# Ranking and expert stages of a graph layer: sums between the halves of a split, TensorE's experts written out, statistics moved to ScalarE

## The reference, cut to what matters

```python
xn = layernorm(x)                                    # x: 6250 nodes x 256
x = x + gnn(xn, src, dst, edge_weight) + mix(xn)     # 100000 edges, sorted by dst
x = x + ffn(layernorm(x))

def gnn(x, row, col, val):       # row = src, col = dst
    agg = segment_sum(val[:, None] * x[col], row, num_segments=6250)
    return agg @ W.T + b

def ffn(x):                      # 8 experts, hidden size 1024, the best 2 of each token
    scores = x @ Wg.T + bg
    combine = softmax over the top 2, 0 for the other experts
    for e in range(8):
        h = relu(x @ W1[e].T + b1[e])
        out += combine[..., e:e+1] * (h @ W2[e].T + b2[e])
```

## Time and profile before

| | |
|---|---|
| median of 3 runs | 2398.07 us (2395.67 to 2400.01) |
| the profiled execution's own time | 2397.73 us |
| its span, first to last instruction | 2395.8 us |
| TensorE busy, share of the span | 1732.4 us, 72% |
| TensorE weight loads | 1202.8 us, 50% |
| VectorE | 1504.8 us, 63% |
| ScalarE | 1248.6 us, 52% |
| GpSimd | 1546.4 us, 65% |
| mean granted TensorE clock | 0.838 of full |

### The profile page before, as it was taken

One profiled execution on the slowest core, in us unless ns is written; L12 is line 12 of the kernel. 1 busy time (PEld: TensorE's weight loads), 2 busy tenths in 40 slices (PEclk: granted clock), 3 DMA queues, 4 the chain that ended last, 5 costly groups with the idle time before them and its releaser, 6 DMA issues. The chain is left out here.

```text
span 2395.8 us, 56194 instructions
## 1 busy us (share of the span) xinstructions
PE 1732.4 (72%) x13448; PEld 1202.8 (50%) x13449; DVE 1504.8 (63%) x3574; ACT 1248.6 (52%) x4045; POOL 1546.4 (65%) x1870
## 2 busy tenths in 40 slices
PE   4876636666666777777666666575899999999994
PEld 2355534444443555555222222365677777777773
DVE  8898826666666776766666676657344544544542
ACT  0044426666666666666666676340455555555552
POOL 3048866777777777777777777104466666666662
PEclk8988868999998999999655555555899999999997
DMA  4012215555555544443333454240222222222224
GB/s 147 1 58 70 68 51 172 156 157 156 152 154 153 152 120 120 121 121 113 104 102 116 142 169 125 93 158 4 51 41 42 42 41 41 43 41 41 42 42 127
DMA packets 140509, 230.72 MB, mean 96 GB/s; under 512 B 33192, under 2 KB 94916, under 8 KB 140214
## 3 DMA queue, kind: packets, MB, share of 16 engines
q0 software_dynamic: 67040, 147.18, 24.5%
q1 hardware_dynamic: 73398, 82.71, 11.1%
HBM read 187.80 MB, written 48.38 MB: 99 GB/s over the span
## 5 line engine op out<-in xcount | busy, mean ns | idle before, releaser
L952 POOL DMA_INDIRECT misc<-z_d,consts x902 | 859.4, 953 | 252.1 <-issue 226.5
L1204 DVE SCALAR_TENSOR_TENSOR acc<-ps,consts,acc 128x256 f32 x902 | 434.8, 482 | 298.7 <-PE ps L1286 281.6
L1675 PE MATMUL ps<-big,rec 128*128 x840 | 314.2, 381 | 39.1 <-DVE rec L1802 33.4
L1284 PE MATMUL ps<-misc 128*128 128x256 f16 x565 | 176.3, 312 | 221.9 <-ACT rec L983 99.9
L1661 PE MATMUL ps<-misc,big 128*128 128x128 f16 x1680 | 324.7, 221 | 0.0
L1659 PE MATMUL ps<-misc,big 128*128 128x128 f16 x1680 | 324.4, 221 | 0.3 <-ACT misc L1773 0.3
L1660 PE MATMUL ps<-misc,big 128*128 128x128 f16 x1680 | 323.1, 220 | 0.0
L1800 DVE CAST rec<-misc 128x512 f16<-128x512 f32 x210 | 98.0, 466 | 342.1 <-ACT misc L1694 269.0
L983 ACT ACTIVATE rec<-rec,misc 128x128 f16<-128x128 f16 x674 | 230.2, 392 | 155.7 <-DVE rec L1065 154.8
L983 ACT ACTIVATE misc<-rec,misc 128x128 f16<-128x128 f16 x678 | 231.4, 392 | 93.5 <-DVE rec L1065 91.4
L1284 PEld LDWEIGHTS ps<-misc 128*128 128x128 f16 x565 | 57.3, 101 | 365.7 <-ACT rec L983 173.1
(11 more groups left out here) (337 smaller groups left out, 3988.5 us busy)
## 6 DMA issues: line engine op xcount, KB each, us to landing
big<-in_w2T SPq DMA_DIRECT2D x60, 256.0 KB, 2.9
misc<-z_d,consts POOLq DMA_INDIRECT x902, 2.8
big<-xT_d SPq DMA_DIRECT2D x98, 128.0 KB
big<-in_w1T SPq DMA_DIRECT2D x32, 256.0 KB, 2.8
tok_d<-misc SPq DMA_DIRECT2D x50, 132.0 KB, 1.7
y_d<-acc SPq DMA_DIRECT2D x50, 128.0 KB, 1.7
xT_d<-misc SPq DMA_DIRECT2D x49, 128.0 KB
z_d<-misc SPq DMA_DIRECT2D x49, 128.0 KB, 1.7
```

Source lines behind the costliest of these rows:

```text
L952: e.indirect_dma_start(out=rows[k], out_offset=None, in_=c.z_d, in_offset=bass.IndirectOffsetOnAxis(ap=idx[u][:, k:k + 1], axis=0)).then_i ...
L1204: e.scalar_tensor_tensor(out=rows_of, in0=out_ps[t % BG], scalar=c.gain, in1=rows_of, op0=ALU.mult, op1=ALU.add).then_inc(s_add[k], 1)
L1284: e.matmul(o, w[:, 0, :], rows[k][:, 0:D], start=True, stop=False)
L1675: l = e.matmul(y_ps[s.u], high[s.u][:, m, :], c.w2[:, bass.ds(at, 2 * D)], start=m == 0, stop=m == HB - 1)
```

## The change

In `rank`: `src` has a semaphore of its own (`s_src`), and VectorE's one-hots wait for it alone; the one-hots and TensorE's counts are written out for 49 blocks. `pick1` is made by ScalarE as a copy of the identity. The statistics of x are made by ScalarE: 49 sums with an accumulator output, a mean by VectorE at block 1 of the places loop, 49 sums of squares, and the remaining steps by VectorE at blocks 42, 45 and 46. The 28 indicators and `started` move to GpSimd, `blk_row` to ScalarE behind the places loop, TensorE's sum for it too. The places have three PSUM buffers instead of two, and the reaches stand at blocks 5, 6, 8, 9 and so on to 45. In `route`, `c.experts` goes. In `experts`, VectorE makes the sums of tile i - 1 between the two halves of tile i; TensorE's program is written out, loads eight expert numbers before every eighth tile, and puts pair m behind group m.

```diff
@@ -233,6 +233,7 @@
+    prefix = [c.wide[u] for u in (1, 2, 0)]
...
@@ -276,11 +279,12 @@
         def _(e):
-            for t, a in inputs:
-                e.dma_start(t[:, 0:EF], a[0:EF * P].rearrange("(p t) -> p t", p=P)).then_inc(s_load, 16)
-            e.wait_ge(s_preset, 3)
-            for t, a in inputs:
-                e.dma_start(t[0:ER, EF:EF + 1], a[EF * P:E].rearrange("(p t) -> p t", t=1)).then_inc(s_load, 16)
+            for n, (t, a) in enumerate(inputs):
+                sem = s_load if n else s_src
+                e.dma_start(t[:, 0:EF], a[0:EF * P].rearrange("(p t) -> p t", p=P)).then_inc(sem, 16)
+                if n == 0:
+                    e.wait_ge(s_preset, 3)
+                e.dma_start(t[0:ER, EF:EF + 1], a[EF * P:E].rearrange("(p t) -> p t", t=1)).then_inc(sem, 16)
...
@@ -320,7 +324,6 @@
-            g.add(e.memset(pick1, 1.0))
...
@@ -337,12 +340,22 @@
-            select(pick1, pick1, ALU.is_equal, 0, [[-1, NT], [0, P]], 1)
...
+            e.wait_ge(s_end, 1)
+            g.sync()
+            e.tensor_scalar(started, tile_no, end[:, 0:1], None, ALU.is_ge).then_inc(s_started, 1)
+            e.wait_ge(s_delta, 1)
+
+            def indicate(n):
+                if n >= 2:
+                    e.wait_ge(s_dest, n - 1)
+                e.tensor_scalar(ind[n % 2], kio, first_run[:, n:n + 1], None, ALU.is_ge).then_inc(s_ind, 1)
+            for n in range(NG):
+                indicate(n)
...
@@ -379,22 +392,18 @@
-            e.wait_ge(s_load, 96)
+            e.wait_ge(s_src, 32)
...
-            with e.Fori(0, NT // 7) as i:
-                for u in range(7):
-                    b = i * 7 + u
-                    e.tensor_scalar(onehot[:, bass.ds(b, 1), :], one(blk16), number[:, bass.ds(b, 1)], None,
-                                    ALU.is_equal).then_inc(s_hot, 1)
+            for b in range(NT):
+                e.tensor_scalar(onehot[:, b, :], blk16, number[:, b:b + 1], None, ALU.is_equal).then_inc(s_hot, 1)
+            e.wait_ge(s_load, 64)
...
-            e.wait_ge(s_x, 32)
-            stats(e, v, c, st, c.mean, var, s_var)
...
@@ -403,9 +412,6 @@
-            e.wait_ge(s_std, 1)
-            v.link(e.reciprocal(c.rstd, std))
-            e.scalar_tensor_tensor(out=c.nbias, in0=c.mean, scalar=-1.0, in1=c.rstd, op0=ALU.mult, op1=ALU.mult).then_inc(s_norm, 1)
...
@@ -424,15 +430,15 @@
-            e.tensor_scalar(started, tile_no, end[:, 0:1], None, ALU.is_ge).then_inc(s_end, 1)
+            e.nop().then_inc(s_end, 1)
...
@@ -442,11 +448,23 @@
-            e.wait_ge(s_row, 1)
-            e.tensor_scalar(blk_row[0:1, :], row[0:1, 0:ET], float(D), None, ALU.mult).then_inc(s_blkrow, 1)
-            e.wait_ge(s_blkrow, 1)
             v.sync()
             e.nop().then_inc(s_base, 1)
+
+            def moments(n):
+                if n == 0:
+                    e.wait_ge(s_sums, 1)
+                    e.tensor_scalar(c.mean, st[:, :, 0], -1.0 / D, None, ALU.mult).then_inc(s_mean, 1)
+                elif n == 1:
+                    e.wait_ge(s_sums, 2)
+                    e.tensor_scalar(var, st[:, :, 1], 1.0 / D, EPS, ALU.mult, ALU.add).then_inc(s_var, 1)
+                elif n == 2:
+                    e.wait_ge(s_std, 1)
+                    v.add(e.reciprocal(c.rstd, std))
+                else:
+                    v.sync()
+                    e.wait_ge(s_mean, 1)
+                    e.tensor_tensor(c.nbias, c.mean, c.rstd, ALU.mult).then_inc(s_norm, 1)
...
@@ -465,16 +483,12 @@
-            def indicate(g):
-                if g >= 2:
-                    e.wait_ge(s_dest, g - 1)
-                e.tensor_scalar(ind[g % 2], kio, first_run[:, g:g + 1], None, ALU.is_ge).then_inc(s_ind, 1)
             for b in range(NT):
                 e.wait_ge(s_pre, b + 1)
-                e.copy_predicated(place, onehot[:, b, :].bitcast(U16), c.wide[b % 2 + 1][:, 0:EC]).then_inc(s_pos, 1)
-                if b < NG:
-                    indicate(b)
-                elif cleared <= b < cleared + 4:
+                e.copy_predicated(place, onehot[:, b, :].bitcast(U16), prefix[b % 3][:, 0:EC]).then_inc(s_pos, 1)
+                if b in (1, 42, 45, 46):
+                    moments((1, 42, 45, 46).index(b))
+                if cleared <= b < cleared + 4:
                     whole(b - cleared)
                 e.wait_ge(s_pos, b + 1)
...
@@ -517,6 +531,34 @@
         def _(e):
+            e.wait_ge(s_k, 2)
+            e.copy(pick1, c.ident[:, 0:NT].rearrange("p (t a) -> p t a", a=1).to_broadcast([P, NT, P])).then_inc(s_pick, 1)
...
+            junk = [matrix(a, 1, D) for a in xn] + [xT[0].rearrange("p h n -> p (h n)").rearrange("p (a d) -> p a d", a=1)]
+
+            def total(sem, n):
+                e.wait_ge(s_mean if n else s_x, 1 if n else 32)
+                e.nop().then_inc(sem, 2)
+                with e.Fori(0, NT // 7) as i:
+                    for u in range(7):
+                        at = bass.ds(i * 7 + u, 1)
+                        to = junk[2 if u == 6 else u % 2]
+                        e.wait_ge(sem, i * 7 + u + 1)
+                        if n == 0:
+                            l = e.activation(to, c.acc3[:, at, :], ACT.Copy, accum_out=st[:, at, 0])
+                        else:
+                            l = e.activation(to, c.acc3[:, at, :], ACT.Square, bias=c.mean[:, at], accum_out=st[:, at, 1])
+                        l.then_inc(sem, 1)
+                e.wait_ge(sem, NT + 2)
+                e.nop().then_inc(s_sums, 1)
+            total(s_sum[0], 0)
+            total(s_sum[1], 1)
+            e.wait_ge(s_scale, 1)
+            e.wait_ge(s_pos, cleared)
+            e.activation(pieces[:, 2, :, :], twice(wgt.bitcast(F32)), ACT.Copy, scale=c.gscale[:, 0:1]).then_inc(s_whi, 1)
+            e.wait_ge(s_int, 2)
+            e.copy(pieces[:, 0, :, :], twice(blk_i)).then_inc(s_piece, 1)
...
@@ -539,17 +581,14 @@
-            e.wait_ge(s_scale, 1)
...
+            e.wait_ge(s_row, 1)
+            e.activation(blk_row[0:1, :], row[0:1, 0:ET], ACT.Copy, scale=float(D)).then_inc(s_blkrow, 1)
             mask(Turn(0, 0))
...
@@ -577,17 +616,14 @@
-            with e.Fori(0, NT // 7) as i:
-                for u in range(7):
-                    b = i * 7 + u
-                    e.wait_ge(s_hot, b + 1)
-                    for x, y in cols:
-                        e.matmul(counts[:, x:y], band[:, bass.ds(P - 1 - b, P)], onehot[:, bass.ds(b, 1), x:y],
-                                 start=False, stop=False)
+            for b in range(NT):
+                e.wait_ge(s_hot, b + 1)
+                for x, y in cols:
+                    e.matmul(counts[:, x:y], band[:, P - 1 - b:2 * P - 1 - b], onehot[:, b, x:y], start=False, stop=False)
             for x, y in cols:
...
@@ -596,9 +632,6 @@
-            e.wait_ge(s_end, 1)
-            e.matmul(row[0:1, 0:512], few[:, 0:1], started[:, 0:512], start=True, stop=True)
-            e.matmul(row[0:1, 512:ET], few[:, 0:1], started[:, 512:ET], start=True, stop=True).then_inc(s_row, 1)
...
@@ -617,13 +650,13 @@
-                if b >= 2:
-                    e.wait_ge(s_pos, b - 1)
+                if b >= 3:
+                    e.wait_ge(s_pos, b - 2)
                 for x, y in cols:
-                    e.matmul(c.wide[b % 2 + 1][:, x:y], c.before, onehot[:, b, x:y], start=True, stop=False)
+                    e.matmul(prefix[b % 3][:, x:y], c.before, onehot[:, b, x:y], start=True, stop=False)
                 for part in (lo16, hi16):
                     for x, y in cols:
-                        l = e.matmul(c.wide[b % 2 + 1][:, x:y], pick1[:, b, :], part[:, x:y], start=False, stop=part is hi16)
+                        l = e.matmul(prefix[b % 3][:, x:y], pick1[:, b, :], part[:, x:y], start=False, stop=part is hi16)
                 l.then_inc(s_pre, 1)
...
@@ -633,10 +666,16 @@
+            e.wait_ge(s_pick, 1)
+            reached = [5 + g * 3 // 2 for g in range(NG)]
             for b in range(NT):
                 places(b)
-                if 1 <= b <= NG:
-                    reach(b - 1)
+                if b in reached:
+                    reach(reached.index(b))
+            e.wait_ge(s_pos, NT)
+            e.wait_ge(s_started, 1)
+            e.matmul(row[0:1, 0:512], few[:, 0:1], started[:, 0:512], start=True, stop=True)
+            e.matmul(row[0:1, 512:ET], few[:, 0:1], started[:, 512:ET], start=True, stop=True).then_inc(s_row, 1)
...
@@ -1309,7 +1348,6 @@
-    c.experts = matrix(pos.take(MT // 4 * 8, I32), MT // 4, 8)
...
@@ -1509,10 +1547,7 @@
-            v.link(e.memset(c.experts, 0))
-            for n in range(5):
-                v.add(e.tensor_copy(c.experts[:, :, n], order[:, n:n + MT - 4:4]))
-            v.add(e.tensor_copy(c.expert, order))
+            v.link(e.tensor_copy(c.expert, order))
...
@@ -1637,7 +1672,7 @@
-    BEHIND = ((), (), (0,), (1,), (2,), (3, 4), (5,), (6, 7))
+    KNOWN = 8
...
@@ -1793,6 +1828,8 @@
+                    if n and not s.zero:
```

(60 more changed lines are left out.)

3 lines of the change are left out of this document (2 added, 1 removed).

## The result

The changed kernel takes 2298.97 us (median of 4 runs, 2297.10 to 2301.28), the kernel before 2397.62 beside it: ratio 0.9589, 95% interval 0.9572 to 0.9605. The forecast was 2299, range 2284 to 2337. The profiled execution took 2297.7 us, its span is 2296.0, 99.8 less than before.

What follows compares the result with a forecast made beforehand. It took a loop between ScalarE and VectorE, 6.48 us a tile, to bound the experts, and VectorE to be ranking's path. 2397.7 - 71 (experts) - 1 (routing) - 27 (ranking) = 2298.7, forecast 2299, range 2284 to 2337.

Steps and rivals of the forecast that it cites:

- rival 6: Experts: the loop between ScalarE and VectorE isn't what bounds, so they stay as they are; -28 alone, 2370 us; chance 0.05.
- rival 4: Experts: GpSimd becomes the bound if its scatter and gather pair took 6.0 us; +36, 2335 us; chance 0.05.
- TensorE's pace: Experts: TensorE becomes the bound at 5.50 us a step, taken from one step that ran without a wait.
- Rival 1: Experts: TensorE's sequencer becomes the bound, each step losing 0.3 us; +31, 2330 us; chance 0.11.
- The load: Experts: loading expert numbers before every eighth tile costs TensorE 0.8 us each time, bounds 0.5 and 1.5.
- 102 x 5.65: Experts: the steps behind the turn at 1703.04, at 5.65 us each, take 576.3 us; with 11.8 before them, 588.1.
- TensorE's order: Experts: products starting after group 0 make a loop through TensorE of 5.0 us, below 5.50.
- What the statistics covered: Ranking: with statistics off VectorE, the gain's transfer and TensorE's transpose come back in part, +0.7 us.
- The wait at block 1: Ranking, places loop: VectorE stalls 5 us for ScalarE's 49 sums, bounds 0 and 18.
- Indicators: Ranking, places loop: GpSimd takes 0.8 us for each indicator of 512 elements, has 1.6, and keeps up.
- Rival 2: Ranking: indicators on GpSimd block VectorE's predicated copies, 28 x 0.8 to 1.5 us, part inside the stall; +20, 2319; chance 0.08.
- rival 5: Experts: written-out TensorE waits for new instructions once a tile, 2.37 us each; +249, slower at 2548 us; chance 0.03.

Runs made afterwards that it cites:

- e4: The changed kernel with the old order of TensorE's products (none behind groups 0 and 1), still written out: 2298.95 us, ratio 0.9573 to the kernel before.
- e9: The kernel before with only TensorE's experts written out, keeping the old order of products: 2396.73 us, ratio 0.9992.

## Why the prediction was right, point by point

- *What bounds the experts.* Right. Moving the sums alone gave 32.2 us (rival 6 is out), and in the changed kernel ScalarE waits for TensorE. GpSimd isn't the bound either (rival 4): it waits for ScalarE 95 times, 104.7 us.
- *TensorE's pace.* The step "so TensorE becomes the bound, at 5.50" was a size off: with computed addresses a step away from the loads is 5.65, and only with fixed ones 5.50. The 5.50 came from one step of the earlier trace rows. Rival 1 named the mechanism with 0.3 us a step; the run with fixed addresses shows 0.15.
- *The load.* Taken 0.8, measured 0.65, within the bounds 0.5 to 1.5. ScalarE's load, 0.4 in eight tiles, is not to be told from the rest of the 0.15. Eight tiles: 45.2 forecast, 45.85 measured.
- *A step too many.* The sum takes "102 x 5.65" behind the turn at 1703.04. That turn is the fourth of 105, so 101 steps follow, and the sum should have been 11.8 + 101 x 5.65 = 582.5 instead of 588.1. Measured: 11.7 to the fourth turn, as forecast, then 101 steps of 5.73, 578.8. The steps were underrated by 101 x 0.08 = 8 us, and the miscount hid 5.65 of them: so the experts came to -68.8, with the tail, against -71.
- *TensorE's order.* That it opens a second loop, through VectorE's split, was right, and that it costs nothing, too (e4). What it costs while the first loop is still the bound was not asked: 7.7 us, by the waits because it releases the relus later.
- *Start and one-hots.* -1.8 and -4.6 were forecast; the first VectorE operation began 3.0 earlier, and the one-hots' first to last start is 17.2 us instead of 22.7, 5.5 less, with none over 1.18 us.
- *What the statistics covered.* The term that failed: "+0.7" for the gain's transfer and TensorE's transpose. The transfer of gnn_wT is queued behind x on SP, lands at 28.4, and VectorE waits 4.55 us for it. Adding the 1.4 us that three operations lose beside GpSimd (28-column product 0.81 for 0.25, cast 1.02 for 0.57, subtraction 1.34 for 0.98), 3.85 + 1.4 - 1.2 - 0.9 = 3.1, where the first predicated copy was 2.8 later than forecast.
- *The wait at block 1.* 5 us forecast, 1.37 measured. Two errors cancel: x landed at 28.2 instead of 24, and a sum took 0.40 us instead of 0.50, 0.10 of it the reading of the accumulator. The sums so ended at 48.2, as forecast (48.5); the wait is short because the copy behind which it stands came 2.8 us late.
- *Indicators.* 0.8 us taken, 0.5 to 1.5 as bounds, 1.56 measured, outside. It cost next to nothing because the reaches come every one and a half blocks, 1.61 us. The sum had a margin of two there; the run has none. Rival 2's other half, blocked predicated copies, didn't happen, with 1.04 us each.
- *Places.* 64.5 forecast, 104.00 - 43.83 = 60.2 measured: 3.6 from the shorter wait, 0.7 from the rest. So the ranking is -29.3 instead of -27; a late start and a short loop cancel.
- *Routing.* -1 was forecast. The experts begin 31.0 us earlier and the places end 29.3 earlier, but the first turns of the changed kernel and of five runs with the same code ahead of them spread over 10 us (1660.2 to 1670.4): not told apart.
- *Supply of instructions* (rival 5). The instruction queue moved 96 packets where it had moved 31, and writing out alone (e9) cost nothing.

That the sum came out to 0.1% is luck. The ranking came out 2 us better and the experts 2 worse. In the ranking, errors of 3 to 4 us stand against each other; in the experts, steps underrated by 8 us stand against a miscount of 5.65. With the steps counted rightly, the forecast would have been 2293.

## What to carry to other kernels

Before an engine's side is written out or reordered, find the loop that bounds it: writing TensorE's side out cost 7.7 us with the new order and gave nothing with the old one while the other loop was the bound, and gave 38 to 42 us once that loop had been shortened. When work leaves an engine, list every transfer that landed under its cover, in the order of the queue that issues them. A lower bound taken from one good step holds for that step's instructions; where addresses are computed or registers loaded, price them apart. Count the steps of a sum by the rows: one too many hid most of an error here.

## What the runs showed of the hardware that was not expected

- Addresses computed from a loaded expert number cost TensorE 0.15 us a tile (2.6%) although no wait of it is shown: the matmuls only stand a little further apart, and the page calls the engine busy.
- A load of registers on TensorE took 0.33 us for four numbers and 0.59 for eight, and lengthened the steps by 0.37 and 0.66. For twenty-one it took 1.6 to 1.8 us at two of five loads and 5.2 to 5.3 at the others, which left TensorE idle for up to 4.94 us, and behind that 4 to 6 us at the 1.2 GHz level.
- An accumulator output of ScalarE is an instruction of its own, 0.19 us long in the trace, 0.10 from one start to the next; the sum of 256 elements with it comes every 0.40 us, the square every 0.50.
- A tensor_scalar on GpSimd over 512 f16 elements takes 1.56 us, while its select over 6272 took 5.89, 3.0 ns an element against 0.94: time per element doesn't carry from one operation to another.
